# GpSimd makes the selection matrix when all rows are normalised, and TensorE waits for it at the first broadcast

## The reference

```python
def block(x, adj, ...):                       # x: 8192 x 128, adj: 8192 x 8192, float32
    h = layernorm(x)
    h = relu(adj @ h @ gcn_w + gcn_b)
    h = layernorm(h) * ln_g + ln_b
    xc, z = split(h @ w_in)                   # 256 channels each
    u = silu(causal_conv4(xc))
    dbc = u @ w_xp                            # dt rank 8, B and C of 16 states
    dt = softplus(dbc[:, :8] @ w_dt + b_dt)
    # 16 states per channel: h_t = exp(dt A) h_(t-1) + dt B u ;  y = sum over states of h_t C
    y = (scan(dt, A, B, C, u) + u * D_skip) * silu(z)
    x = x + y @ w_out
    return x + lstm_attention(layernorm(x))   # LSTM over the 8192 rows, selected prefix sums
```

## Time and profile before

| | us |
|---|---|
| median of 3 runs | 1649.15 (1646.19 to 1650.54) |
| the profiled execution | 1649.25 |
| its span, first to last instruction | 1647.4 |
| TensorE busy | 1534.2 |
| VectorE busy | 1437.4 |
| GpSimd busy | 1114.7 |
| ScalarE busy | 980.2 |

### The profile page before, as it was taken

How to read it: one execution, slowest core, us unless ns; L and a number is a source line. 1 busy time by engine, 2 the same in 40 slices (tenths; PEclk the granted TensorE clock), 3 DMA queues, 4 the chain that set the end, 5 groups by cost and what they waited for, 6 DMA issues and landing times.

```text
span 1647.4 us, 18204 instructions
## 1 busy us (share of the span) xinstructions
PE 1534.2 (93%) x5212; PEld 794.1 (48%) x5212; DVE 1437.4 (87%) x1640; ACT 980.2 (60%) x2051; POOL 1114.7 (68%) x518
## 2 busy tenths in 40 slices
PE   6999999999999999999999999999967669999994
PEld 2444444444444444444444444444422227999993
DVE  8406999999999999999999999999987894558998
ACT  2254766667575766666676757576657444555552
POOL 4014998989898988989898989889867860001221
PEclk9999999999999999999999999999978898999997
DMA  8977767777777777777777777777500203000002
GB/s 309 358 241 263 272 232 254 251 244 257 246 251 258 246 253 242 255 250 247 250 256 240 250 263 241 251 255 253 183 13 8 89 7 109 0 0 1 0 0 102
DMA packets 62649, 317.17 MB, mean 193 GB/s; under 512 B 6898, under 2 KB 6898, under 8 KB 29684
## 3 DMA queue, kind: packets, MB, share of 16 engines
q1 hardware_dynamic: 49680, 293.30, 51.2%
q10 hardware_dynamic: 12900, 23.08, 4.8%
HBM read 304.03 MB, written 12.32 MB: 192 GB/s over the span
## 4 chain that ended last, share of the span: by engine, by line
PE 62%; DVE 24%; issue 9%; ACT 2%; POOL 1%; DVEq 1%; ACTq 0%; DMA 0%; POOLq 0%
PE bank L526 39%; DVE work L1143 11%; PE bank L446 10%; PE bank L451 4%; DVE work L1093 4%; PE bank L555 3%; PE bank L571 3%; DVE work L1166 2%; DVE work L1101 1%; PE bank L562 1%; PE bank L564 1%; DVE work L1197 1%; DVE work L1065 1%; POOL work L943 1%; DVE work L1202 1%
## 5 line engine op out<-in xcount | busy, mean ns | idle before, releaser
L526 PE MATMUL bank<-ring,xh 128*128 128x512 f32 x2048 | 951.8, 593 | 15.8 <-DVE xh L1031 15.8
L1143 DVE TENSOR_TENSOR_SCAN work<-bank,hstate,work 128x512 f32<-128x512 f32 x512 | 627.7, 1267 | 17.0 <-ACT bank L787 12.7
L526 PEld LDWEIGHTS bank<-ring,xh 128*128 128x128 f32 x2048 | 389.4, 190 | 463.3 <-issue 436.8
L922 POOL TENSOR_TENSOR work<-work 128x1024 f32<-128x1024 f32 x210 | 502.7, 2394 | 88.2 <-DVE work L1101 82.6
L787 ACT ACTIVATE bank<-work,a_neg 128x512 f32<-128x512 f32 x512 | 346.8, 687 | 303.1 <-DVE work L1143 302.3
L1093 DVE TENSOR_TENSOR work<-work,bank 128x1024 f32<-128x1024 f32 x256 | 309.9, 1215 | 26.6 <-PE bank L451 16.0
L446 PE MATMUL bank<-work,w_sb 128*128 128x512 f32 (+2 forms) x352 | 181.8, 614 | 20.4 <-ACT work L777 10.2
L993 POOL TENSOR_TENSOR work<-work 128x256 f32 x32 | 28.5, 891 | 240.1 <-ACT work L826 240.1
L1101 DVE TENSOR_TENSOR work<-work,bank 128x1024 f32<-128x1024 f32 x154 | 184.2, 1196 | 1.3
L451 PE MATMUL bank<-bc_parts,sel 96*128 96x512 bf16 x442 | 168.2, 391 | 16.0 <-DVE work L1093 7.0
L882 POOL TENSOR_TENSOR work<-work 128x1024 f32<-128x1024 f32 x48 | 113.6, 2367 | 80.9 <-ACT work L679 80.7
(11 more groups left out here) (144 smaller groups left out, 1635.8 us busy)
## 6 DMA issues: line engine op xcount, KB each, us to landing
ring<-adj_t SPq DMA_DIRECT2D x256, 1024.0 KB, 4.9
work<-c_scratch ACTq DMA_DIRECT2D x35, 256.0 KB, 4.4
c_two<-c_scratch ACTq DMA_DIRECT2D x35, 256.0 KB, 4.3
xh<-x_rows SPq DMA_DIRECT2D x16, 256.0 KB, 5.9
work<-x_t SPq DMA_DIRECT2D x16, 256.0 KB, 5.1
x_scratch<-work ACTq DMA_DIRECT2D x16, 256.0 KB, 5.1
work<-x_scratch SPq DMA_DIRECT2D x1, 4096.0 KB, 13.6
out_t<-work SPq DMA_DIRECT2D x16, 256.0 KB, 2.7
```

The lines of the kernel that those rows point to most:

```text
L526: last = nc.tensor.matmul(mixed[:, :], xn[:, j, :], a, start=(j == 0), stop=(j == BLK - 1))
L922: nc.gpsimd.tensor_tensor(out=acc, in0=hc[0] if n == 1 else acc, in1=hc[n % 2], op=ALU.add).then_inc(y_added, 1)
L1143: nc.vector.tensor_tensor_scan(hb[s % 2][:, h, :], da[h], dbu[s % 2][:, h, :], hstate[:, HV * s + h:HV * s + h + 1], ALU.mult, ALU.add).th ...
```

## The change

GpSimd's memset and three selects for `sel` move from the head of its queue to behind `less_first`, and get a wait for all 16 row groups (`xn_ready`, XG = 16) ahead of them. TensorE's wait for `sel` moves from the head of step 1 to the first broadcast, in slot 14 of step 1. Nothing is computed differently.

```diff
@@ TensorE, head of step 1
                     pe.wait_ge(consts_in, 32)
                     pe.wait_ge(consts_ready, 1)
-                    pe.wait_ge(sel_ready, 4)
                     pe.wait_ge(cen_ready, 2)
@@ TensorE, spread_b
                     if s >= DS - 2 and pre:
                         n = s - (DS - 2)
+                        if k == 1 and n == 0:
+                            pe.wait_ge(sel_ready, 4)
                         if n == 0:
@@ GpSimd
-            nc.gpsimd.memset(sel[:, :], 0.0).then_inc(sel_ready, 1)
-            view = sel[:, :].rearrange("p (n m) -> p n m", m=P)
-            for g in range(PARTS):
-                pool.wait_ge(sel_ready, g + 1)
-                nc.gpsimd.affine_select(out=view, in_=view, compare_op=ALU.not_equal, fill=1.0, base=-BC * g,
-                                        pattern=[[-1, BC], [0, P]], channel_multiplier=1).then_inc(sel_ready, 1)
             nc.gpsimd.memset(cen_w[:, :], -1.0 / D).then_inc(cen_ready, 1)
...
             nc.gpsimd.memset(less_first[:, 0:1], 0.0).then_inc(fold_ready, 1)
+            pool.wait_ge(xn_ready, XG)
+            nc.gpsimd.memset(sel[:, :], 0.0).then_inc(sel_ready, 1)
+            view = sel[:, :].rearrange("p (n m) -> p n m", m=P)
+            for g in range(PARTS):
+                pool.wait_ge(sel_ready, g + 1)
+                nc.gpsimd.affine_select(out=view, in_=view, compare_op=ALU.not_equal, fill=1.0, base=-BC * g,
+                                        pattern=[[-1, BC], [0, P]], channel_multiplier=1).then_inc(sel_ready, 1)
             pool.wait_ge(consts_in, 32)
```

## The result

| | before | changed |
|---|---|---|
| median | 1649.15 us (7 runs, 1643.79 to 1651.39) | 1642.43 us (7 runs, 1640.73 to 1643.63) |
| ratio, 95% interval | | 0.9961 (0.9946 to 0.9976) |
| span of the profiled execution | 1647.4 us | 1641.7 us |

The two profiled executions differ by 5.7 us in span; that of the changed kernel (1643.63 us) is the slowest of its seven runs. Lines that stood at L1031, L1021, L1019, L1017 and L1036 are L1033, L1023, L1021, L1019 and L1038 here; L526 is L527, L451 is L450.

What follows compares the result with a forecast made beforehand. It took VectorE's stalled first rows, then TensorE through chunk 0, as the bound. Span 1647.4 us less 5.8 at the start, 0 for transfers and moved work, plus 1.85 gave 1643.4 us; range 1641.3 less 0.3 to 1646.8 us.

Steps and rivals of the forecast that it cites:

- What holds VectorE: First row groups: GpSimd's three selects lock the shared port and stall three VectorE instructions, 7.95 us in all.
- Rival E: Kernel start: the long VectorE instructions belong to the start itself and stay, 1649.2 us, chance 0.08.
- The start: Chunk 0: TensorE starts at 9.9 us, piece 1 moves from 21.11 to 15.3 us, a gain of 5.8 us.
- Rival D: Piece 0: TensorE's clock stays at 1.2 GHz throughout, a gain of 4.4 us, 1644.8 us, chance 0.11.
- Rival B: Kernel start: first piece lands sooner than its row says, the whole 7.9 us count, 1641.3 us, chance 0.07.
- The cover of the transfers: Chunk 0: adjacency pieces land 2.9 us early at piece 4, 0.6 us at piece 13, so no stall.
- rival C: Chunk 0: transfers hold TensorE, a stall of 1.5 us (up to 2.5), 1644.9 us, chance 0.13.
- The rows: Chunk 0: VectorE needs 2.91 us per row group against TensorE's 3.43 us, so rows win 0.5 us per piece.
- The moved work: Selection matrix made after the rows, 58.4 to 74.5 us: sums to 0, L1036 held by 2.91 us without harm.
- Where it would turn bad: GpSimd's moved block costs nothing unless it takes over 68 us, and outweighs the gain over 74 us.
- rival F: First broadcast: TensorE waits for a late matrix, slower if the block takes over 74 us instead of 16, chance 0.03.
- The sum: Whole kernel: 1647.4 us span less 5.8, with 1.85 us around it, 1643.4 us for the profiled execution.

Runs made afterwards that it cites:

- experiments 1: Changed kernel without GpSimd's wait for the rows, so the matrix is made at once: 1650.85 us median, ratio 1.0012 to the kernel before.
- experiment 2: Changed kernel with GpSimd waiting for 8 row groups instead of 16, selects amid the normalising: 1651.93 us median, ratio 1.0018 to the kernel before.
- edit A: Changed kernel with the first adjacency piece issued ahead of row group 1: 1642.80 us median, ratio 0.9952 to the kernel before.
- experiment 4: Changed kernel with a second read of each of the row groups 2 to 15, to a scratch tensor: 1648.17 us (one run).

## Why the prediction was right, and where its steps were off

- **What holds VectorE.** Right. All three stalls are gone, and experiments 1 and 2 show that such stalls follow GpSimd's block wherever it goes. Rival E falls with them.
- **The start.** The gain at the mark was 5.82 us, the predicted 5.8, but out of errors that cancel, which is luck. The first piece landed at 9.5 us instead of 9.9 and TensorE started at 9.56 us; piece 0 took from there to 15.6 us, 6.0 us instead of 5.4, since the clock rose 5.0 us after the first matmul (loads 0.85 us apart until 13.96 us) and not 3.4 us. The 0.3 us that are left came back because piece 1's first load stands at 14.96 us, ahead of piece 0's end, where the prediction's sum lets piece 1 begin at that end. The size that one row gave for the clock's rise was the weak term: in the other profiles of the changed start it took 3.3 to 5.8 us, counted to the first short load. Rival D was half there, and its price is in the result.
- **Rival B** (no wait for the first piece) had its landing more often than its 0.07 says, but not its gain. The landing took 7.8 us in this profile and 7.9 to 8.2 in others, but 6.1 us in experiment 2 and 6.7 us with the selects made four times, where TensorE started at 8.10 and 8.54 us. Even so the mark moved by 6.7 us in the second of these and by 6.85 us with edit A (start at 8.12 us), and not by 7.9 us, the slow clock taking its part of piece 0. A landing read once is one draw.
- **The cover of the transfers.** Wrong in size. Piece 13 was issued at 46.49 us, landed 7.1 us later and was needed at 15.0 + 12 x 3.43 = 56.2 us, so it was 2.6 us early where the prediction had 0.6. Piece 4 (issued at 15.59 us, 7.0 us) had been 2.7 us early: the cover did not melt. The step that was off is "the cover melts by 2.1 us in 8 pieces, 0.26 us each", which took the 359 and 379 GB/s of the earlier trace rows for what the queues can do, while they were about what was asked. With 420 GB/s shown in experiment 4, rival C had no case at this demand. The 425 GB/s of the Trainium skill ("HBM Reference", section "Specifications (TRN2)"), which the prediction set aside, agree with the 420 GB/s measured there.
- **The rows.** That the rows "win 0.5 us per piece" was wrong too: VectorE waits for its row groups' transfers, and all rows were done at 58.6 us, as predicted (58.4) only because the kernel before had those waits as well. It did no harm.
- **The moved work.** Right: 0. L1038 lost 2.5 us (the prediction named 2.91), and the block ended at 74.1 us (predicted 74.5).
- **Where it would turn bad.** Wrong. That the part costs nothing "unless the block takes over 68 us", and rival F with its 74 us, counted only who waits for the matrix. A block of 51 us (twelve selects) already cost 17 us (one run), because the tap additions are queued behind it. In the changed kernel GpSimd idles for 17.3 us before them, and with the selects made twice the unit that they feed is ready at 99.8 us for a projection at 104.6 us, another 4.9 us; with the block's own 15.4 us that puts the limit at 38 us, an estimate that was not itself run.
- **The sum.** 1643.4 us predicted for the profiled execution, 1643.63 us measured, the slowest of seven; the median of 1642.43 us lies 1 us lower, within the scatter (1640.73 to 1643.63).

## What to carry to other kernels

A select or a memset of 3.5 to 4 us on GpSimd costs VectorE's chain at the moment where it stands, so one-off tables belong where VectorE has nothing that is due, and the test is to compare the slowest instance of each repeated VectorE instruction with its median. When a stall is taken away, look for what else was hidden behind it (here a transfer and a slow clock), and when work is moved, price everything that is queued behind it and not only the reader of its product.

## What the runs showed of the hardware

- A select (96 x 4096, bfloat16) held VectorE's two-SBUF-input product, its subtraction and its 128 x 4 scale until its end (the product 4.32 us in experiment 2 and the subtraction 4.23 us in the kernel before, instead of 0.69; the scale 3.08 us instead of 0.17). The memset of the same tile held the scale (1.99 and 1.76 us instead of 0.17). Reductions and a product with a PSUM operand were not held (0.67 to 0.69 us).
- TensorE's clock fell in idle gaps of 3.55 us (granted 0.58 from 20 to 27 us), 4.96 us (0.73 from 8 to 13 us) and 13.45 us (0.57 from 110 to 125 us), and in experiment 2 just after one of 1.88 us (loads 0.85 us apart from 40.99 us). It did not fall at the 2.66 us of the kernel before, nor at the 3.28 us of experiment 2, where loads are 0.43 us apart behind the gap: the length of the gap alone doesn't tell. The slow matmuls cost another 2.6 us behind the gap of 3.55 us, 2.8 behind that of 13.45 and 1.8 behind that of 1.88.
- The first adjacency piece, 1 MB, landed 7.8 to 8.2 us after its issue in eight profiles with the same order of issues, and 6.1 and 6.7 us in two.
